# The block scales of the gate and up weight rows in a PSUM bank in place of SBUF

## Chip, cores, metric

One NeuronCore of a Trainium2 chip runs the whole program in one launch. The metric is the time of one execution on the device in microseconds (us). Float32 inputs and outputs; products are made of bfloat16 halves.

## What is computed

x is 4 x 2048 x 512. Each of the 8192 rows passes two blocks:

```
x = x + attention(layernorm(x), ctx, ctx)      # 16 heads of 32, 77 keys per batch, padding mask, weights 512 x 512
x = x + fp4_linear(silu(fp4_linear(n, w_gate)) * fp4_linear(n, w_up), w_down)     # n = layernorm(x), inner width 1408
def fp4_linear(x, w): return fp4(x) @ fp4(w).T
def fp4(v):                                    # blocks of 16 along the last dimension
    scale = max(max(abs(block)) / 6, 1e-12)
    return nearest of (0, .5, 1, 1.5, 2, 3, 4, 6) to abs(block / scale), with its sign, * scale
```

So the weights w_gate and w_up (1408 x 512 each) and w_down (512 x 1408) must be rounded once, block by block, and transposed, before the tiles of 128 rows of x can use them.

## The kernel before

**Stages.** There is a preparation (0 to 68 us) in which the attention weights, keys, values and w_down are transposed and rounded; a stretch (68 to about 190 us) in which the 11 pairs of gate and up rows (128 rows each of w_gate and w_up, index i) are rounded while the attention of the first tiles already runs; then a pipeline over the 64 tiles of 128 rows, whose steps repeat to the end. Each engine has one instruction queue, whose order is written out by hand; engines meet by semaphores alone.

**One pair of rows, i.** SyncE loads 128 x 512 of w_gate and of w_up into the two halves of `raw` (L319 to L321); it issues the load of pair i+1 once VectorE has divided both halves of pair i (semaphore `w_val`). VectorE's `weight_front(i)` does for both halves (two "jobs", alternating) `top` (L1258, the largest magnitude of each of the 32 blocks of 16), `scale` (L1264, a sixth of it), `inverse` (L1274, its reciprocal), and then `divide` (L1278: raw times the reciprocal, spread over each block, into `hv`). Each step of a job waits for the step before it of the same job. ScalarE's `weight_grid` squares the result (L926) and adds a large constant, by which it is rounded (L934). VectorE's `weight_end(i, half)` repeats the scale into a row of its own, `result_scale` (L1269), and subtracts (L1320). GpSimd's `weight_end` subtracts once more (L560) and multiplies by that last scale (L564), into `hq`. TensorE transposes `hq` (L715) into PSUM bank 0 or 1, ScalarE copies it out as the high bfloat16 half (L973), VectorE's `gate_up_low` takes the low half (L1246, wguT<-psum). L1246 is the line of a helper, `low`, which many steps use: `half_low` (halves<-...) and `probabilities_low` (p_h<-probs,p_h) too.

The scales stand in `w_sc` (SBUF, 128 x 2 jobs x 4 rows x 44 blocks): row 0 the largest magnitudes, 1 the scale, 2 the reciprocal, 3 the scale for GpSimd. The rows of w_down, in the preparation, use it too.

**What stands between.** VectorE's queue from 68 us on mixes the 11 fronts and 22 ends with the steps of tiles 0 to 3: statistics of the normalisation (L1390, L1394), `q_low` (L1399, L1402), `maximum` of the scores (L1432), `probabilities_low`, `normalised` (L1407, L1411), `half_low`, `residual` (L1448, x_new). The transposes between the stages go by DMA from SyncE's queue (t_room<-halves). TensorE starts the pipeline's gate and up products when the last low half of the weights is there.

**PSUM.** Eight banks of 128 x 512 float32. Bank 6 (`down_ps`) takes one of eight turns in the preparation, and from tile step 2 on the output of the last product; between the two nothing uses it.

Of the kernel before, what the change touches and what calls it, by code (L numbers as in the profile page):

```python
# [16 lines left out]
FP4_BLOCK = 16  # L17
# [8 lines left out]
def at_least(eng, sem, value):  # L26

    if not isinstance(value, int) or value > 0:
        eng.wait_ge(sem, value)
# [5 lines left out]
Job = namedtuple("Job", "name source src val sq mag tot res sc nb divided squared done")  # L35
# [29 lines left out]
def xattn_fp4_ffn_kernel(nc, x, ctx, mask, wq, bq, wk, bk, wv, bv, wo, bo, w_gate, w_up, w_down, out):  # L65
    BATCH, SEQ, D = x.shape
# [4 lines left out]
    KC = D // P  # L71
# [15 lines left out]
    HALF = INNER // 2  # L87
# [14 lines left out]
    with ExitStack() as es:  # L102
        def sb(name, shape, dt=F32):
            return es.enter_context(nc.sbuf_tensor(name, shape, dt))
# [11 lines left out]
        pv_ps = psum[:, 2:6, 0:GROUPS * VW].rearrange("p r (g w) -> p r g w", g=GROUPS)  # L116
        down_ps = bank[6]
        q_bank = o_bank = bank[7]
        quarter = [slice(r * DK, (r + 1) * DK) for r in range(GH)]


# [52 lines left out]
        w_sc = sb("w_sc", [P, 2, 4, HALF // FP4_BLOCK])  # L174
# [64 lines left out]
        fills = [entry for entry in plan if entry[0] not in ("quant", "round")]  # L239
# [413 lines left out]
        def _(pe):  # L653
# [10 lines left out]
            for n, (kind, what) in enumerate(fills):  # L664
                ps = bank[n % 8]
                at_least(pe, prep_lo, n - 7)
                if kind == "weight":
                    which, _, kc = what
                    if which not in waited:
                        waited.add(which)  # L670
# [570 lines left out]
        def _(dve):  # L1241
            own = Steps(dve, dve_step)

            def low(dst, ps, high, signal, value):

                return own.did(dve.tensor_tensor(dst, ps, high, ALU.subtract), signal, value)  # L1246
# [19 lines left out]

            def result_scale(job):

                own.did(dve.tensor_scalar(job.sc[:, 3, 0:job.nb], job.sc[:, 0, 0:job.nb], 1.0 / 6.0,  # L1269
                                          SCALE_FLOOR, ALU.mult, ALU.max))  # L1270

            def inverse(job):
# [3 lines left out]
            def divide(job):  # L1276
                own.after(marks[job.name])
                step_of(job, dve.scalar_tensor_tensor(blocks(job.val), blocks(job.src), TIES_DOWN, spread(job.sc, 2, job.nb),  # L1278
                                                      ALU.mult, ALU.mult), job.divided)
# [12 lines left out]
                step_of(job, dve.tensor_tensor(blocks(job.res), blocks(job.tot), spread(job.sc, 1, job.nb), ALU.mult),  # L1292
                        job.done)

            def weight_job(name, cols, divided, squared, done):
                part = [t[:, cols] for t in (raw, hv, h_sq, hm, hs, hq)]
                return Job(name, None, *part, w_sc[:, name], (cols.stop - cols.start) // FP4_BLOCK,
                           divided, squared, done)

            def weight_jobs(width, before):  # L1300

                return [weight_job(s, slice(s * width, (s + 1) * width),
                                   *((sem, before + (s + 1)) for sem in (w_val, w_grid, w_sum)))
                        for s in range(2)]

            def weight_start(jobs, before):

                at_least(dve, w_sum, before)
                for step in (top, scale, inverse):
                    for job in jobs:  # L1310
                        step(job)
                for job in jobs:
                    divide(job)

            def weight_sum(job, before):

                at_least(dve, w_quant, before - 1 + job.name)
                result_scale(job)
                dve.wait_ge(*job.squared)
                own.did(dve.tensor_tensor(job.tot, job.mag, job.val, ALU.subtract), *job.done)  # L1320


            n = 0
            for kind, what in plan:
                if kind == "quant":
                    dve.wait_ge(w_loaded, 16 * (what + 1))
                    weight_start(weight_jobs(HALF, 2 * what), 2 * what)
                    continue
                if kind == "round":
                    for job in weight_jobs(HALF, 2 * what):  # L1330
                        weight_sum(job, 2 * what)
                    continue
                if kind == "keys" and what == 0:
                    dve.wait_ge(bias_loaded, 16 * 3)
                    own.did(dve.tensor_scalar(bk_col[:], bk_col[:], SM_SCALE, None, ALU.mult), bk_ready, 1)
                ps = bank[n % 8]
                dve.wait_ge(prep_hi, n + 1)
                if kind == "weight":
                    which, dst, kc = what
                    own.did(dve.scalar_tensor_tensor(dst[:, LO, kc, :], ps[:], fill_scale[which], dst[:, HI, kc, :],  # L1340
                                                     ALU.mult, ALU.subtract), prep_lo, n + 1)
                elif kind == "ctx":
                    low(ctxT[:, LO, what], ps[:, 0:BATCH * KEYS], ctxT[:, HI, what], prep_lo, n + 1)
                elif kind == "keys":
                    own.did(dve.scalar_tensor_tensor(
                        k_all[:, :, LO, what, :], ps[:, 0:BATCH * KEYS].rearrange("p (b k) -> p b k", b=BATCH),
                        bk_col[:, what:what + 1], k_all[:, :, HI, what, :], ALU.add, ALU.subtract), prep_lo, n + 1)
                elif kind == "values":
                    low(v_all[:, what, LO, :, 0:DK], ps[0:KEYS, :].rearrange("p (h d) -> p h d", d=DK),
                        v_all[:, what, HI, :, 0:DK], prep_lo, n + 1)  # L1350
                elif kind == "down":
                    i, m = what
                    ks, cols = h_fills[m], slice(i * P, (i + 1) * P)
                    low(wdT[:, LO, ks.start:ks.stop, cols],
                        ps[:, 0:len(ks) * P].rearrange("p (k n) -> p k n", k=len(ks)),
                        wdT[:, HI, ks.start:ks.stop, cols], prep_lo, n + 1)
                else:
                    dve.wait_ge(bo_loaded, 16)
                    own.did(dve.tensor_tensor(bo_all[:], bo_all[:], wo_bv, ALU.add), prep_lo, n + 1)
                n += 1  # L1360
# [6 lines left out]
                    wguT[:, half, HI, :, cols], w_lo, 2 * i + half + 1)  # L1367

            def gate_up_jobs(i):
                return weight_jobs(D, 2 * i + 2 * KC)  # L1370

            def weight_front(i):

                dve.wait_ge(w_loaded, 32 * i + 16 * KC + 32)
                weight_start(gate_up_jobs(i), 2 * i + 2 * KC)

            def weight_end(i, half):
                weight_sum(gate_up_jobs(i)[half], 2 * i + 2 * KC)
# [9 lines left out]
            def first_norm(m):  # L1388
                dve.wait_ge(x_loaded, 16 * m + 16)
                marks["norm1"] = own.did(dve.bn_stats(ln1_stats_sb, x_in))  # L1390
# [73 lines left out]
            def step(e, d, f, a, b, n, m):  # L1464
# [62 lines left out]
                    h_chunk(f, 3)  # L1527
                own.restart()

            weight_front(0)  # L1530
            first_norm(0)
            first_norm_end(0)
# [228 lines left out]
```

## Time and profile before

| what | us |
|---|---|
| three timed runs | 2031.81, 2033.88, 2034.55; median 2033.88 |
| the profiled execution, its own time | 2031.19 |
| its span, first to last instruction | 2029.3 |
| TensorE busy | 1898.9 (94%) |
| VectorE busy | 1770.0 (87%) |
| ScalarE busy | 1266.9 (62%) |
| GpSimd busy | 448.8 (22%) |

The rows are of the profiled execution; 1.9 us of its time lie outside the span. Engines: PE is TensorE's matmuls, PEld its weight loads, DVE VectorE, ACT ScalarE, POOL GpSimd, SP SyncE. L1278 is line 1278 of the kernel. "out<-in" are the kernel's names; where a row names h_room, it is one of the tensors hv, hm, hs, hq that lie in it. A duration reaches from an instruction's start to the acknowledgement of its last write, so that two neighbours on one engine overlap by some 0.08 us. The idle time of an engine before an instruction is in brackets, with what ended it.

### The profile page before, as it was taken

The numbers are of one execution on the slowest core, as the hardware profiler recorded it, in microseconds if no ns is written. First come the engines' busy times: TensorE is split into PE (matmuls) and PEld (weight loads), VectorE is DVE, ScalarE is ACT, GpSimd is POOL, SyncE is SP. The second block draws the span as 40 slices with busy tenths as digits, with TensorE's granted clock in tenths as the row PEclk, the third lists the DMA queues.
The fourth block names the chain that finished last, engine by engine and source line by source line (L and its number), as shares of the span: only waits on it lengthen the run. The fifth ranks groups of instructions, "written<-read, shape, count | busy, mean of one in ns | idle before, by whom it ended". The sixth has DMA issues, their size and how long they took to land.

```text
span 2029.3 us, 48669 instructions
## 1 busy us (share of the span) xinstructions
PE 1898.9 (94%) x17724; PEld 1192.0 (59%) x17792; DVE 1770.0 (87%) x2676; ACT 1266.9 (62%) x2613; POOL 448.8 (22%) x526
## 2 busy tenths in 40 slices
PE   6446899999999999999999999999999999999987
PEld 4334566656665666656665666666665666666643
DVE  7898889888899889888899889888899889888874
ACT  4575766676666666676666666676667666676421
POOL 5554221122112221122112211222112211222100
PEclk8667999999999999999999999999999999999998
DMA  5344566565766566566666566556765566556623
GB/s 170 105 114 95 109 144 144 127 132 132 156 133 132 130 145 139 129 133 134 149 138 132 130 147 138 127 134 136 154 131 132 130 149 137 126 134 133 128 56 84
DMA packets 716996, 265.34 MB, mean 131 GB/s; under 512 B 667930, under 2 KB 669878, under 8 KB 716958
## 3 DMA queue, kind: packets, MB, share of 16 engines
q1 hardware_dynamic: 715374, 264.85, 58.9%
q8 instruction: 22, 0.36, 0.1%
q10 hardware_dynamic: 1584, 0.01, 0.1%
q14 instruction: 16, 0.13, 0.0%
HBM read 66.34 MB, written 34.86 MB: 50 GB/s over the span
## 4 chain that ended last, share of the span: by engine, by line
PE 86%; DVE 6%; DMA 3%; issue 2%; POOL 1%; SPq 1%; ACT 1%; DVEq 0%; POOLq 0%; another core or an unknown queue 0%; ACTq 0%
PE psum L724 44%; PE psum L660 38%; PE psum L737 2%; PE psum L766 2%; DMA t_room<-halves 1%; DVE h_room L1278 1%; SPq L345 1%; PE psum L755 1%; POOL h_room L560 1%; DVE w_sc L1258 1%; POOL h_room L564 1%; DMA ph_room<-h_room 1%; DVE wguT L1246 1%; DVE h_room L1320 0%; DMA q_room<-in_L_xattn_Wk_dram 0%
## 5 line engine op out<-in xcount | busy, mean ns | idle before, releaser
L724 PE MATMUL psum<-wguT,t_room 128*128 128x352 bf16 x6144 | 943.1, 314 | 15.5 <-DVE h_room L1426 9.0
L724 PEld LDWEIGHTS psum<-wguT,t_room 128*128 128x128 bf16 x6144 | 597.4, 98 | 346.4 <-DVE h_room L1426 10.4
L660 PE MATMUL psum<-wdT,ph_room 128*128 128x512 bf16 x2108 | 469.8, 381 | 11.2 <-DMA ph_room<-h_room 10.9
L581 POOL TENSOR_TENSOR ln_var_eps<-ln_mean_var,eps 128x1 f32<-128x1 f32 x128 | 103.8, 811 | 1185.7 <-DVE ln_mean_var L1394 998.6
L660 PEld LDWEIGHTS psum<-wdT,ph_room 128*128 128x128 bf16 x2112 | 207.6, 98 | 263.3 <-issue 17.4
L982 ACT ACTIVATE silu_g<-psum 128x352 f32<-128x352 f32 x256 | 117.4, 459 | 380.2 <-PE psum L724 377.1
L988 ACT ACTIVATE probs<-psum,neg_max 128x77 f32<-128x77 f32 x1024 | 244.3, 350 | 3.7 <-DVE neg_max L1432 3.0
L1426 DVE TENSOR_TENSOR h_room<-silu_g,psum 128x352 f32<-128x352 f32 x256 | 132.2, 517 | 81.3 <-ACT silu_g L982 81.1
L1019 ACT ACTIVATE t_room<-psum,bq_col 128x128 bf16<-128x128 f32 x256 | 72.9, 367 | 185.7 <-PE psum L660 185.7
L660 PE MATMUL psum<-t_room,wqT 128*128 128x128 bf16 x3072 | 187.6, 222 | 0.8 <-DMA t_room<-halves 0.8
L660 PEld LDWEIGHTS psum<-t_room,wqT 128*128 128x128 bf16 x3072 | 177.7, 100 | 1.5 <-DMA t_room<-halves 1.1
L660 PE MATMUL psum<-woT,t_room 128*128 128x512 bf16 x705 | 165.7, 384 | 12.0 <-issue 10.1
L926 ACT ACTIVATE h_sq<-h_room 128x1408 bf16<-128x1408 f32 (+2 forms) x94 | 108.1, 1150 | 96.3 <-DVE h_room L1278 96.3
L595 POOL TENSOR_TENSOR io_room<-io_room,bo_all 128x512 f32<-128x512 f32 x64 | 81.7, 1276 | 239.7 <-DMA io_room<-in_x_dram 239.7
L660 PEld LDWEIGHTS psum<-woT,t_room 128*128 128x128 bf16 x768 | 70.7, 99 | 84.3 <-issue 4.4
L1448 DVE TENSOR_TENSOR x_new<-psum,io_room 128x512 f32<-128x512 f32 x64 | 44.2, 691 | 81.9 <-PE psum L660 74.0
L1278 DVE SCALAR_TENSOR_TENSOR h_room<-h_room,h_sc 128x1408 f32<-128x1408 f32 x64 | 104.5, 1633 | 2.1
L1292 DVE TENSOR_TENSOR h_room<-h_room,h_sc 128x1408 f32<-128x1408 f32 x64 | 104.0, 1625 | 2.1
L1246 DVE TENSOR_TENSOR h_room<-h_room 128x1408 bf16<-128x1408 f32 x64 | 103.6, 1619 | 1.4 <-ACT h_room L1059 1.4
L1246 DVE TENSOR_TENSOR p_h<-probs,p_h 128x624 bf16<-128x624 f32 x128 | 103.9, 812 | 0.0
L1288 DVE SCALAR_TENSOR_TENSOR h_room<-h_sq,h_room 128x1408 f32<-128x1408 bf16 x64 | 103.6, 1618 | 0.1
L1258 DVE TENSOR_REDUCE h_sc<-h_room 128x88 f32<-128x1408 f32 x64 | 102.6, 1603 | 0.1
(105 smaller groups left out, 2498.8 us busy)
## 6 DMA issues: line engine op xcount, KB each, us to landing
io_room<-in_x_dram SPq DMA_DIRECT2D x128, 256.0 KB, 2.8
x_scratch<-x_new SPq DMA_DIRECT2D x64, 256.0 KB, 2.0
x_cur<-x_scratch SPq DMA_DIRECT2D x64, 256.0 KB, 3.3
out_dram<-io_room SPq DMA_DIRECT2D x64, 256.0 KB, 2.4
t_room<-halves SPq DMA_TRANSPOSE x192, 3.2
raw<-in_L_ffn_w_down_dram SPq DMA_DIRECT2D x4, 704.0 KB, 4.3
raw<-in_L_ffn_w_gate_dram SPq DMA_DIRECT2D x11, 256.0 KB, 2.7
raw<-in_L_ffn_w_up_dram SPq DMA_DIRECT2D x11, 256.0 KB, 2.9
```

Of the source, the lines that this page charges most:

```text
L581: own.did(pool.tensor_tensor(var_eps, mean_var[:, 1:2], eps[:], ALU.add))
L660: ins = pe.matmul(dst, left(i), right(j), start=first and n == 0, stop=last and n == len(PRODUCTS) - 1)
L724: ins = pe.matmul(ps[:, 0:CW], left[:, i, kc, :], wguT[:, which, j, kc, cols], start=(kc == 0 and i == j), stop=(kc == KC - 1 and i == LO))
L926: act.activation(dst, val, ACT.Square, scale=GRID_SLOPE).then_inc(done, 1)
L982: act.activation(silu_g[:, c % 2, :], gate_ps[c][:, 0:CW], ACT.Silu).then_inc(silu_done, 1)
L988: ins = act.activation(probs[:, h, 0:KEYS], score_ps[:, r, g, :], ACT.Exp, bias=neg_max[:, h:h + 1])
L1246: return own.did(dve.tensor_tensor(dst, ps, high, ALU.subtract), signal, value)
L1258: step_of(job, dve.tensor_reduce(job.sc[:, 0, 0:job.nb], blocks(job.src), AX_X, ALU.max, apply_absolute_value=True))
L1278: step_of(job, dve.scalar_tensor_tensor(blocks(job.val), blocks(job.src), TIES_DOWN, spread(job.sc, 2, job.nb), ALU.mult, ALU.mult), job.d ...
L1288: step_of(job, dve.scalar_tensor_tensor(job.tot, job.sq, GRID_BASE, job.tot, ALU.add, ALU.subtract))
L1292: step_of(job, dve.tensor_tensor(blocks(job.res), blocks(job.tot), spread(job.sc, 1, job.nb), ALU.mult), job.done)
L1426: own.did(dve.tensor_tensor(h[:, c * CW:(c + 1) * CW], silu_g[:, c % 2, :], up_ps[c][:, 0:CW], ALU.mult), h_done, f * CHUNKS + (c + 1))
```

## The change

The rows 0, 1 and 2 of the scales of gate and up rows move to bank 6 of PSUM, as `row_sc` (128 x 2 jobs x 3 rows x 32 blocks). Row 3, which GpSimd reads, stays in `w_sc`. The rows of w_down stay as they are. Before the first front, VectorE waits for the last fill of the preparation, since bank 6 was in use there.

```
+        row_sc = down_ps[:, 0:2 * 3 * (D // FP4_BLOCK)].rearrange("p (n r k) -> p n r k", n=2, r=3)
...
             def result_scale(job):
-                own.did(dve.tensor_scalar(job.sc[:, 3, 0:job.nb], job.sc[:, 0, 0:job.nb], 1.0 / 6.0,
+                own.did(dve.tensor_scalar(w_sc[:, job.name, 3, 0:job.nb], job.sc[:, 0, 0:job.nb], 1.0 / 6.0,
                                           SCALE_FLOOR, ALU.mult, ALU.max))
...
-            def weight_job(name, cols, divided, squared, done):
+            def weight_job(name, scales, cols, divided, squared, done):
                 part = [t[:, cols] for t in (raw, hv, h_sq, hm, hs, hq)]
-                return Job(name, None, *part, w_sc[:, name], (cols.stop - cols.start) // FP4_BLOCK,
+                return Job(name, None, *part, scales[:, name], (cols.stop - cols.start) // FP4_BLOCK,
                            divided, squared, done)
-            def weight_jobs(width, before):
-                return [weight_job(s, slice(s * width, (s + 1) * width),
+            def weight_jobs(scales, width, before):
+                return [weight_job(s, scales, slice(s * width, (s + 1) * width),
...
-                    weight_start(weight_jobs(HALF, 2 * what), 2 * what)
+                    weight_start(weight_jobs(w_sc, HALF, 2 * what), 2 * what)
...
-                    for job in weight_jobs(HALF, 2 * what):
+                    for job in weight_jobs(w_sc, HALF, 2 * what):
...
             def gate_up_jobs(i):
-                return weight_jobs(D, 2 * i + 2 * KC)
+                return weight_jobs(row_sc, D, 2 * i + 2 * KC)
...
+            dve.wait_ge(prep_lo, len(fills))
             weight_front(0)
```

## Rows read from the trace of the kernel before

**Rows 1.** The page: busy us, share of the span and count of each engine.

```profile
PE 1898.9 (94%) x17724; PEld 1192.0 (59%) x17792; DVE 1770.0 (87%) x2676; ACT 1266.9 (62%) x2613; POOL 448.8 (22%) x526
```

**Rows 2.** Windows: length, then busy us of each engine, clock, DMA.

```profile
68.00:182.00 114.00, 52.16 (x574) 39.06 (x576) 111.22 (x216) 72.19 (x160) 67.44 (x60) 0.63 0.41 97
230.00:1960.00 1730.00, 1711.87 (x16289) 1070.61 (x16349) 1536.34 (x2281) 1120.54 (x2315) 336.46 (x418) 1.00 0.62 134
```

**Rows 3.** Chain of waits, 68 to 182 us, shares by line.

```profile
by line: DVE h_room L1278 16.6%; DVE w_sc L1258 11.0%; DVE wguT L1246 9.0%; DVE h_room L1320 7.9%; DVE w_sc L1264 6.1%; DMA raw<-in_L_ffn_w_up_dram 5.3%; DVE w_sc L1274 4.5%; DVE halves L1246 4.4%; issue 4.4%; PE psum L660 4.3%; DMA t_room<
```

**Rows 4.** VectorE's groups, 68 to 180 us: busy us, mean ns, idle before.

```profile
L1278 DVE SCALAR_TENSOR_TENSOR h_room<-raw,w_sc 128x512 f32<-128x512 f32 x22 | 20.9, 991 | 0.0
L1320 DVE TENSOR_TENSOR h_room<-h_room 128x512 f32<-128x512 f32 x22 | 15.0, 680 | 0.4 <-ACT h_room L934 0.4
L1246 DVE TENSOR_TENSOR wguT<-psum,wguT 128x512 bf16<-128x512 f32 x22 | 14.7, 673 | 0.0
...
L1264 DVE TENSOR_SCALAR w_sc<-w_sc 128x32 f32<-128x32 f32 x22 | 8.7, 435 | 0.0
L1269 DVE TENSOR_SCALAR w_sc<-w_sc 128x32 f32<-128x32 f32 x22 | 6.5, 296 | 0.0
```

**Rows 5.** Timeline of VectorE, first front: start, us taken.

```profile
68.53 1.27 DVE L1258 TENSOR_REDUCE w_sc<-raw 128x32 f32<-128x512 f32 x2
69.72 0.30 DVE L1264 TENSOR_SCALAR w_sc<-w_sc 128x32 f32<-128x32 f32 x2
...
70.41 1.22 DVE L1278 SCALAR_TENSOR_TENSOR h_room<-raw,w_sc 128x512 f32<-128x512 f32 x2
71.55 0.69 DVE L1390 BATCH_NORM_STATS2 ln_stats<-io_room 128x6 f32<-128x512 f32 x1
```

**Rows 6.** Timeline, third front (i = 2), VectorE and GpSimd.

```profile
84.52 1.06 POOL L564 TENSOR_TENSOR h_room<-h_room,w_sc 128x512 f32<-128x512 f32 x1
84.77 0.93 DVE L1264 TENSOR_SCALAR w_sc<-w_sc 128x32 f32<-128x32 f32 x2
...
86.13 2.71 DVE L1278 SCALAR_TENSOR_TENSOR h_room<-raw,w_sc 128x512 f32<-128x512 f32 x2
86.90 1.39 POOL L564 TENSOR_TENSOR h_room<-h_room,w_sc 128x512 f32<-128x512 f32 x1
```

**Rows 7.** Timeline behind the front of i = 7, VectorE and GpSimd.

```profile
135.72 1.72 POOL L595 TENSOR_TENSOR io_room<-io_room,bo_all 128x512 f32<-128x512 f32 x1
136.22 1.28 DVE L1246 TENSOR_TENSOR wguT<-psum,wguT 128x512 bf16<-128x512 f32 x2
```

**Rows 8.** Timeline, 142 to 153 us: L1269 of i = 7, and x_new.

```profile
142.14 1.03 DVE L1269 TENSOR_SCALAR w_sc<-w_sc 128x32 f32<-128x32 f32 x1
...
152.48 0.69 DVE L1448 TENSOR_TENSOR x_new<-psum,io_room 128x512 f32<-128x512 f32 x1 [1.17 <-PE psum L660]
```

**Rows 9.** Chain of waits, 142 to 153 us: start, us.

```profile
142.33 4.76 DMA t_room<-halves
147.54 4.92 PE psum L660 x11
```

**Rows 10.** VectorE's groups, 230 to 1960 us.

```profile
L1292 DVE TENSOR_TENSOR h_room<-h_room,h_sc 128x1408 f32<-128x1408 f32 x60 | 97.5, 1625 | 2.0
L1399 DVE SCALAR_TENSOR_TENSOR t_room<-psum,bq_col,t_room 128x128 bf16<-128x128 f32 x177 | 51.2, 345 | 21.9 <-ACT t_room L1019 21.9
L1274 DVE RECIPROCAL h_sc<-h_sc 128x88 f32<-128x88 f32 x61 | 42.3, 694 | 0.1
L1274 DVE RECIPROCAL x_sc<-x_sc 128x32 f32<-128x32 f32 x61 | 21.5, 353 | 2.1
L1407 DVE RECIPROCAL inv_sum<-psum 128x16 f32<-128x16 f32 x60 | 15.4, 257 | 0.8 <-PE psum L737 0.8
```

**Rows 11.** ScalarE's groups, 68 to 180 us.

```profile
L934 ACT ACTIVATE h_room<-h_sq 128x512 f32<-128x512 bf16 x22 | 13.9, 630 | 0.7
L1026 ACT ACTIVATE psum<-mask_raw 128x1232 f32<-128x1232 uint8 x4 | 4.9, 1226 | 0.0
```

## The prediction

> **What bounds the kernel now.** I read the page first. VectorE is busy 87% of the span and GpSimd 22% [rows 1], but those are averages over stages with different limits. The windows part them. From 230 to 1960 us TensorE is busy 1711.9 of 1730 us: it is the bound there, and nothing that VectorE gains in that stage would move the end. The edit does nothing there anyway. From 68 to 182 us, where the gate and up rows are rounded, VectorE is busy 111.2 of 114 us and TensorE only 52.2 [rows 2]. The chain of waits says the same with names: in that stretch it runs over L1278, L1258, L1246, L1320, L1264, all VectorE, with two loads of raw and a piece of TensorE between [rows 3]. So a microsecond taken off VectorE in this stretch moves the start of the pipeline, and with it the end, unless another wait has taken its place by then.
>
> The groups of VectorE show what is odd in it. L1264 works on 32 numbers per partition and takes 435 ns on average; L1278 on 512 numbers takes 991 ns, where L1320 of the same width takes 680 [rows 4]. The timeline explains it. In the first front GpSimd has no rounding work yet: two L1264 take 0.30 us, two L1278 1.22 us, and the front is 71.55 - 68.53 = 3.02 us long [rows 5]. In the third front the pair of L1264 starts at 84.77, while GpSimd's L564 runs until 84.52 + 1.06 = 85.58, and ends at 85.70; the pair of L1278 starts at 86.13 and is over at 88.84, 0.55 us after the L564 that ends at 88.29 [rows 6]. The last of each kind that was held is finished its own length, or a little more, after a GpSimd instruction ends. An instruction of VectorE whose tensors all lie in SBUF is held until GpSimd's current one is done. Not so with a tensor in PSUM: two wguT<-psum take 1.28 us right within GpSimd's 135.72 to 137.44 [rows 7], and all 22 of them average 673 ns, as fast as the undisturbed L1320 [rows 4]. L1258 and L1274 are not held in any front.
>
> **What it removes.** All 11 fronts stand in the timeline of the same view as rows 5 and 6. From the first L1258 to the start of what follows the last L1278 they take, in order, 3.02, 4.99, 5.18, 4.24, 4.82, 3.65, 4.42, 5.35, 3.65, 3.92 and 3.26 us. The ten behind the first exceed it by 13.3 us in all. The groups give the same: 22 x (991 - 650) ns = 7.5 us for L1278 (two undisturbed ones span 1.22 us with an overlap of 0.08, so 650 ns each) and 22 x (435 - 175) = 5.7 us for L1264 [rows 4, 5]. With the reciprocals in PSUM, L1278 has one tensor in SBUF as input and one in PSUM, as the wguT row has; L1264 has none in SBUF. So all of the 13.3 us goes from where it stands.
>
> L1269 is held too (22 x (296 - 170) = 2.8 us) and also frees itself, but I cost this at nothing: L1320 stands right behind it with both inputs in SBUF, and it will be held in its place. The L1269 of rows 8 takes 1.03 us and is over at 143.17, when GpSimd has just finished, and the L1320 behind it runs free; with the edit L1320 waits for that same end.
>
> **What comes back.** GpSimd's four instructions per pair take about 4.7 us and begin when the first L1320 of a pair ends; the front that overlaps them will be over 1 us before them. What then follows matters. I went through the fronts one by one, moving each by the sum gained so far. i = 1: half_low (both inputs in SBUF) is held by the last L564; of 1.97 us I keep 1.76. i = 2: half_low follows directly and is held 1.6 us more; of 2.16 I keep 0.55. i = 3: 1.19 of 1.22. i = 4, 5, 6: statistics, maxima and wguT follow, which read PSUM or one tensor, or probabilities_low at a time when GpSimd is free: all of 1.80, 0.63 and 1.40. i = 7: the two probabilities_low land within GpSimd's L595 and wait for ScalarE's casts as well; of 2.33 I keep 1.5. i = 8: beside it runs another way to x_new, from half_low of tile 0's o: a DMA of 4.76 us, and TensorE's projection takes 4.92 us, and VectorE already waits 1.17 us for that at x_new [rows 8, 9]; so what VectorE gains between 142 and 152 us (0.63 us) only makes this wait longer. i = 9, 10: 0.90 and 0.24 us. Sum: 1.76 + 0.55 + 1.19 + 1.80 + 0.63 + 1.40 + 1.5 + 0 + 0.90 + 0.24 = 9.97, say 10.0 us. The loads of raw move with the divides that release them, so they hide nothing and cost nothing.
>
> **What it adds.** 8 instructions per front and 2 per pair of ends now touch PSUM, 110 in all. No instruction of VectorE writes PSUM in this trace, so its price must be bounded. Low end: nothing. Reading PSUM at 512 elements costs no more than SBUF (673 against 680 ns, rows 4). The reciprocal takes 353 ns for 32 and 694 ns for 88 numbers, 6.1 ns each, so 16 in SBUF would take 256 ns, and 16 read from PSUM take 257 [rows 10]. For writing, only ScalarE has rows: 630 ns for 512 elements into SBUF, 1226 for 1232 into PSUM; the difference is 596 ns for 720 elements, 0.83 each, which leaves 206 ns of fixed time in both [rows 11]. High end: the short L1399, 128 elements, 345 ns. From L1320 (512 elements, 680 ns) and L1292 (1408, 1625 ns) an element costs 945 / 896 = 1.055 ns; that leaves a fixed part of 345 - 135 = 210 for L1399, against 680 - 540 = 140 for L1320, 0.07 us more, though L1399 has a per-partition operand besides [rows 4, 10]. I take 0.02 us per instruction, near the reciprocal's row, the only other small operation: 110 x 0.02 = 2.2 us; between nothing and 7.7 us. The added wait at 68.5 us stands in an idle-free place behind the last wdT fill and exposes its acknowledgement, the overlap of two neighbours: 0.08 us, as between 69.80 (68.53 + 1.27), where L1258 ends, and 69.72, where L1264 starts [rows 5]. TensorE and ScalarE don't touch bank 6 in the stretch.
>
> Net: 10.0 - 2.2 - 0.1 = 7.7 us. Against the profiled execution's 2031.2 that is 2023.5. That one lies at the low end of the times; from the median of 2033.9 the forecast is 2026.2 us.
>
> A rule speaks against the edit. The Trainium skill, "VectorE: DVE Perf Modes", in its section on the TRN2 errata, puts VectorE's fixed part at 58 cycles from SBUF and 120 from PSUM; 62 cycles at 0.96 GHz are 65 ns, an estimate of 7.1 us for 110 instructions, and a gain of 2.8 us, 2031.1, in place of 7.7. The rows of reads at 16 and 512 elements disagree with it; for writes no row decides.
>
> **Rivals.**
> (a) Small operations on PSUM pay the high end, 0.07 us: 110 x 0.07 = 7.7 us, net 10.0 - 7.7 - 0.1 = 2.2 us, 2031.7. For it: L1399. Against it: the reciprocal from PSUM. Chance 0.13. The rule above would bring this case.
> (b) The gain is given back more often than I counted: each front's early end meets GpSimd's chain or a wait for ScalarE at the next step, as in i = 2 and 7. With half of the kept 10 us: 5 - 2.3 = 2.7 us, 2031.2. Against it: in i = 3 to 6 the steps behind read PSUM. Chance 0.08.
> (c) The edit doesn't free L1278: with raw in SBUF it is held like before, and only L1264 gains. L1264's share is 5.7 of 13.2 us, so 4.3 of the 10 us would remain, less 2.3: 2.0 us, 2031.9. Against it: wguT<-psum,wguT, which has one tensor in SBUF too. Chance 0.04.
> (d) Slower: a write into PSUM is acknowledged late, and here each step waits for the one before it (L1258 to L1264 to L1274 to L1278), with nothing but the other job between. In rows 5 the second L1264 follows the end of the second L1258 at once, so there is no slack to hide it in. From 0.09 us per instruction (9.9 / 110) on the change is a loss; at 0.13, nearly twice (a)'s price, it costs 14.3 us, 4.4 more than the 9.9: 2038.3. Against it: ScalarE's rows 11. Chance 0.07.
>
> **How the numbers follow.** My own case has 0.68. Its gain lies between 10.0 - 0.1 - 0 = 9.9 and some 4.5 (0.05 us each). The timed runs here lie up to 2.7 us apart, so 0.2% (4.1 us) is about what can be told from no change. The range reaches from 2022.0, the gain with PSUM free and a little of L1269 and of the last fronts added, over (a), (b) and (c) to 2033.0; beyond it are (d) and a little more. Faster by over 0.2%: my case but for its weak end (0.65), and those ends of (a) and (b) that gain more, 0.68. Within: the rest of my case, (a), (b) and (c), 0.25. Slower: (d), 0.07.
>
> **What would show it.** L1278 at about 650 ns, L1264 at 180 to 220, all fronts 3.0 to 3.4 us long though GpSimd works beside them; half_low behind the front of i = 2 held by about 1.2 us; some L1320 held at over 1 us where L1269 was; more than 1.17 us of idle time before x_new at 152 us; GpSimd's L564 nearer to 1.06. The pipeline's first gate and up product would start 7 to 8 us earlier than 190.4, and everything behind it would keep its distance. The forecast is wrong if fronts are over 3.6 us long (rivals a and d), if L1278 still shows 1.5 us (c), or if the fronts are short and the pipeline doesn't start earlier (b).

## The result, and the profile after

The changed kernel takes 2020.26 us (median of 4 runs, 2019.79 to 2022.32), the kernel before 2033.05 (4 runs beside it, 2031.81 to 2034.55): a ratio of 0.9939 with a 95% interval of 0.9922 to 0.9956. That is 12.8 us or 0.6% less where 7.7 were forecast, and 1.7 us below the low end of the range. Line numbers behind the added line are one higher than before: L1279 is what L1278 was, L1265 was L1264, and so on.

The page after, first of it the span, then the engines' busy time against [rows 1]:

```profile
span 2017.9 us, 48669 instructions
...
PE 1894.5 (94%) x17724; PEld 1189.1 (59%) x17792; DVE 1758.7 (87%) x2676; ACT 1266.9 (63%) x2613; POOL 446.9 (22%) x526
```

The profiled execution's time is 2019.79 us. Its span is 11.4 us shorter than the 2029.3 of before, and VectorE is busy 11.3 us less. The windows, against [rows 2]; the first one now ends where the rounding does, at 169.2:

```profile
68.00:169.20 101.20, 48.85 (x574) 37.18 (x576) 99.51 (x216) 72.00 (x160) 65.50 (x60) 0.66 0.46 109
230.00:1950.00 1720.00, 1702.40 (x16128) 1063.79 (x16186) 1528.27 (x2267) 1112.63 (x2300) 334.20 (x414) 1.00 0.62 134
```

The same 216 instructions of VectorE take 99.5 us in place of 111.2, and the stretch that holds them is 101.2 us in place of 114. The pipeline behind is what it was: TensorE fills 99% of it. VectorE's groups in the stretch, 68 to 167.2 us, against [rows 4] (busy us, mean ns, idle before):

```profile
L1321 DVE TENSOR_TENSOR h_room<-h_room 128x512 f32<-128x512 f32 x22 | 17.3, 788 | 0.5 <-ACT h_room L935 0.4
L1247 DVE TENSOR_TENSOR wguT<-psum,wguT 128x512 bf16<-128x512 f32 x22 | 14.8, 676 | 0.0
L1259 DVE TENSOR_REDUCE psum<-raw 128x32 f32<-128x512 f32 x22 | 14.1, 684 | 1.1 <-DMA raw<-in_L_ffn_w_up_dram 0.7
L1279 DVE SCALAR_TENSOR_TENSOR h_room<-raw,psum 128x512 f32<-128x512 f32 x22 | 13.9, 674 | 0.0
...
L1275 DVE RECIPROCAL psum<-psum 128x32 f32<-128x32 f32 x22 | 6.2, 330 | 0.0
L1270 DVE TENSOR_SCALAR w_sc<-psum 128x32 f32<-128x32 f32 x22 | 3.9, 177 | 0.0
...
L1265 DVE TENSOR_SCALAR psum<-psum 128x32 f32<-128x32 f32 x22 | 3.6, 194 | 0.0
```

L1279 fell from 991 to 674 ns, L1265 from 435 to 194, L1270 from 296 to 177. L1321 rose from 680 to 788: part of L1270's hold stands there now. All eleven fronts are 3.05 to 3.15 us long, and their sum fell from 46.5 to 33.9 us. One of the four executions of one_column_psum, in the table below, took 3982.78 us and is left out of its median.

In the chain of waits behind the stretch, the block of 72 gate and up products that follows the first h_chunk starts 12.6 us earlier than the 190.41 of before (24 such products stand ahead of that h_chunk in both kernels):

```profile
177.81 12.23 PE psum L725 x72
```

### The profile page after: what moved, and what is told of

Same layout as the page of the kernel before. It is cut to its first block, busy times and chain, and to the rows that moved or that the text cites. A ratio compares the mean times of both kernels' runs of the same rounds, so it can differ in the third digit from the quotient of the medians.

```text
span 2017.9 us, 48669 instructions
## 1 busy us (share of the span) xinstructions
PE 1894.5 (94%) x17724; PEld 1189.1 (59%) x17792; DVE 1758.7 (87%) x2676; ACT 1266.9 (63%) x2613; POOL 446.9 (22%) x526
## 4 chain that ended last, share of the span: by engine, by line
PE 85%; DVE 6%; DMA 3%; issue 2%; POOL 1%; SPq 1%; ACT 1%; DVEq 0%; POOLq 0%; another core or an unknown queue 0%; ACTq 0%
PE psum L725 43%; PE psum L661 37%; PE psum L738 2%; PE psum L767 2%; DMA t_room<-halves 1%; SPq L346 1%; PE psum L756 1%; POOL h_room L561 1%; DVE h_room L1321 1%; DVE psum L1259 1%; POOL h_room L565 1%; DVE h_room L1279 1%; DMA ph_room<-h_room 1%; DMA q_room<-in_L_xattn_Wk_dram 0%; DVE wguT L1247 0%
## 5 line engine op out<-in xcount | busy, mean ns | idle before, releaser
L661 PE MATMUL psum<-wdT,ph_room 128*128 128x512 bf16 x2108 | 469.9, 381 | 11.1 <-DMA ph_room<-h_room 10.9
L1279 DVE SCALAR_TENSOR_TENSOR h_room<-h_room,h_sc 128x1408 f32<-128x1408 f32 x64 | 104.8, 1638 | 2.2
```

Of the source, the lines that this page charges most:

```text
L661: ins = pe.matmul(dst, left(i), right(j), start=first and n == 0, stop=last and n == len(PRODUCTS) - 1)
```

## The experiments

Each stretch below is read from that run's timeline: from the start of the first front to the start of the first h_chunk (L1426 before), 68.53 to 189.83 us in the kernel before, so 121.30. The rest is the span less that second start. Times are medians, with the ratio to the kernel before run beside them (2032.38, 2032.26 and 2032.62 us in the three sets).

```
kernel           us       ratio (95%)              stretch  11 fronts  rest
before           2033.05  1                        121.30   46.5       1839.5
after            2020.26  0.9939 (0.9922, 0.9956)  108.64   33.9       1840.7
before_again     2031.58  0.9999 (0.9990, 1.0008)  122.10   46.0       1838.8
after_again      2021.43  0.9946 (0.9933, 0.9960)  108.69   33.9       1840.9
recip_only       2022.06  0.9952 (0.9938, 0.9966)  113.02   39.4       1837.5
max_only         2028.26  0.9980 (0.9971, 0.9989)  118.57   42.2       1841.5
one_column_sbuf  2010.54  0.9893 (0.9878, 0.9908)  100.62   33.7       1842.0
one_column_psum  2011.28  0.9903 (0.9885, 0.9921)  101.28   34.3       1841.0
wait_only        2031.87  1.0000 (0.9990, 1.0009)  121.32   46.0       1841.2
down_too         2022.21  0.9952 (0.9939, 0.9966)  108.75   33.8       1841.2
split_before     2026.99  0.9972 (0.9960, 0.9984)  115.40   40.6       1841.1
split_after      2014.76  0.9917 (0.9904, 0.9931)  106.31   33.9       1837.4
quarter_after    2020.92  0.9941 (0.9928, 0.9955)  112.17   33.9       1837.9
front8_sbuf      2020.84  0.9948 (0.9933, 0.9964)  110.25   34.4       1840.2
```

### Both kernels again

> The kernel before, unchanged, profiled a second time. It tells how much of the 12.6 us by which the pipeline started earlier in the changed kernel is chance. Theory (the way has its own fixed length): from the end of half_low of tile 0's o to the start of x_new (L1448) it takes 10.3 us again, as in the first profile (142.22 to 152.48), and the wait of 1.2 us before x_new is there again; the first silu product h_chunk (L1426) starts at 189.8 within 0.5. Rival (its length varies by itself, with the landing of the DMA transpose and the clock that TensorE is granted at that moment): 8.4 to 10.3 us, and the pipeline starts up to 2 us earlier. Time 2033 in both within 1.5.

> The changed kernel, unchanged, profiled a second time. Fixed way: from the end of half_low of tile 0's o to x_new 8.4 us again (131.96 to 140.33) and no wait before x_new; first h_chunk (L1427) at 177.2 within 0.5; time 2020.3. Rival (length varies by itself): up to 10.3 us, x_new waits, and the first h_chunk starts up to 1.8 us later, time up to 2022.3. Where both repeat, the shorter way belongs to the changed kernel and has a cause in it.

The two differ by 10.2 us here (by 11.0 from the other runs of the kernel before in this set) and by 12.8 in the first set, while their stretches differ by 13.41 and 12.66. So the size of the gain is known to one or two microseconds. The stretch repeats within 0.1 us for the changed kernel and 0.8 for the other; front8_sbuf below shows that it can also move by 1.1 us with nothing changed. Both sets lie above the forecast's 7.7. The idle time before x_new is there again in before_again (1.75 us) and again missing in after_again; before_again's first h_chunk came at 190.75, outside of the expected 189.8 within 0.5.

### One step alone in PSUM

The rows of the scales are picked one by one: recip_only has the reciprocals (row 2, what L1278 reads) in PSUM, max_only the block maxima (row 0, what L1264 and L1269 read). The edit of recip_only, against the changed kernel; max_only has (0,) in place of (2,):

```diff
+            def gate_up_scales(name):
+                return Rows([(row_sc if row in (2,) else w_sc)[:, name, row] for row in range(3)])
...
-                return weight_jobs(row_sc, D, 2 * i + 2 * KC)
+                return weight_jobs(gate_up_scales, D, 2 * i + 2 * KC)
```

> Only the reciprocals (row 2) stand in PSUM; the largest magnitudes and the scale stay in SBUF. Hold theory (an instruction whose tensors all lie in SBUF waits for GpSimd's current instruction, no other): L1278's like falls to 675 ns, L1264's like stays held once per front (mean 400 to 480 ns), fronts 3.5 to 4.2 us long, gain about 7.5 / 13.2 of 12.6 us: 7 us, time 2026. Rival (the saved time meets GpSimd's chain at the next step, as the prediction had it): gain under 4 us, time over 2029.

> Only the largest magnitudes (row 0) stand in PSUM; scale and reciprocal in SBUF. L1264's and L1269's likes then read PSUM and aren't held (under 220 ns), L1278's like is as before. Shares simply add: gain 5.7 / 13.2 of 12.6 us = 5.4 us, time 2027.6. Hold theory in full: the freed L1264 lets L1278 start earlier into the same GpSimd instruction or the one before, so part of the hold only moves to it: L1278's like over 1000 ns, fronts 4.0 to 4.6 us, gain 2 to 4 us, time 2029 to 2031.

VectorE's groups of recip_only, 66.8 to 168 us:

```profile
L1289 DVE SCALAR_TENSOR_TENSOR h_room<-raw,psum 128x512 f32<-128x512 f32 x22 | 13.9, 673 | 0.0
...
L1275 DVE TENSOR_SCALAR w_sc<-w_sc 128x32 f32<-128x32 f32 x22 | 8.6, 430 | 0.0
```

and of max_only, 66.8 to 175 us:

```profile
L1289 DVE SCALAR_TENSOR_TENSOR h_room<-raw,w_sc 128x512 f32<-128x512 f32 x22 | 22.2, 1049 | 0.0
L1337 DVE TENSOR_TENSOR h_room<-h_room 128x512 f32<-128x512 f32 x22 | 17.4, 790 | 0.4 <-ACT h_room L945 0.4
...
L1275 DVE TENSOR_SCALAR w_sc<-psum 128x32 f32<-128x32 f32 x22 | 3.5, 185 | 0.0
```

Each step is freed by the place of its own operand: the divide falls to 673 ns with its scales in PSUM although raw stays in SBUF, so rival (c) is out. The shares aren't equal: the divide's alone shortens the stretch by 8.3 us against the 121.3 of the profile before, the maxima's alone by 2.7. In max_only the divide is held longer than before (1049 against 991 ns), since it comes up earlier, while GpSimd is still at work. In its third front the divides come up at 83.76 and are over at 86.24, 0.55 us after the L571 of GpSimd that runs from 83.97 to 85.69. What is freed first in a row of steps hands part of its hold to the next one.

The timed runs part the two kernels less well than the stretches do. recip_only's median is 10.3 us below the kernel before where 7 were expected, and 0.6 above the changed kernel, though its stretch is 4.3 us longer than that one's. Its profiled execution (2019.32 us) was the fastest of its five, with a rest 3 us shorter than the changed kernel's; the last section has one cause of that. max_only's 4.1 us stand beside 2.7 of stretch, within the 2 to 4 that were expected where a hold moves on.

### No GpSimd beside the fronts: the price of PSUM alone

GpSimd's subtraction and product of the rounding work on one column in place of 512; the other 511 columns of the rounded values are left out. In one_column_sbuf the scales are in SBUF, in one_column_psum in PSUM.

```diff
             def gate_up_end(i, half):
...
+                col = slice(half * D, half * D + 1)
...
+                own.did(pool.tensor_tensor(hs[:, col], hm[:, col], hs[:, col], ALU.subtract), w_sub, at)
...
+                own.did(pool.tensor_tensor(hq[:, col], hs[:, col], w_sc[:, half, 3, 0:1], ALU.mult), w_quant, at)
```

> Leaves out: GpSimd's subtraction and multiplication of the gate and up rows are done on one column of 512 alone. GpSimd then hardly works in the stretch, and all scales stand in SBUF. Theory (holds by GpSimd's current instruction are the whole excess): L1264's like 170 to 185 ns, L1278's 650 to 675, all fronts 3.0 to 3.1 us long with the scales in SBUF. Rival (part of the excess is something else, such as loads or ScalarE): fronts stay over 3.3 us in places. Since half_low, p_h and L1320 are not held either, the first h_chunk comes earlier than in the changed kernel: 13 + 5 us before 189.8.

> Leaves out the same, with the scales in PSUM as in the changed kernel. No hold is left in either, so the difference of the two is the bare price of the 110 instructions on PSUM. Theory (price about 0.007 us each, from the first front: 3.09 against 3.01 us): 0.8 us later at the first h_chunk. The prediction's 0.02 us each: 2.2 us. The rule's 0.065 us each: 7.1 us.

VectorE's groups of one_column_sbuf, 68.5 to 160 us:

```profile
L1288 DVE SCALAR_TENSOR_TENSOR h_room<-raw,w_sc 128x512 f32<-128x512 f32 x22 | 13.5, 653 | 0.0
...
L1274 DVE TENSOR_SCALAR w_sc<-w_sc 128x32 f32<-128x32 f32 x22 | 3.7, 198 | 0.0
```

and of one_column_psum, 67 to 160 us:

```profile
L1289 DVE SCALAR_TENSOR_TENSOR h_room<-raw,psum 128x512 f32<-128x512 f32 x22 | 13.9, 674 | 0.0
...
L1275 DVE TENSOR_SCALAR psum<-psum 128x32 f32<-128x32 f32 x22 | 3.6, 194 | 0.0
```

Two things follow. With the scales in SBUF, and GpSimd nearly out of the way, the fronts are 3.0 us each but for one of 3.53 (33.7 in all). In that one the small steps meet the addition of 512 columns, L605, which GpSimd still does in this kernel:

```profile
119.18 1.26 POOL L605 TENSOR_TENSOR io_room<-io_room,bo_all 128x512 f32<-128x512 f32 x1
119.81 0.76 DVE L1274 TENSOR_SCALAR w_sc<-w_sc 128x32 f32<-128x32 f32 x2
```

They are over 0.13 us after it. So the excess of 13 us was the hold by GpSimd, all of it. And the pair differs by 101.28 - 100.62 = 0.66 us of stretch for 110 instructions: 0.006 us each, and less than two profiles of one kernel can differ by. Reading the 32 reciprocals, each spread over 16 numbers, from PSUM makes the divide 21 ns longer. The 62 cycles that the Trainium skill gives as the difference of the fixed part between a source in SBUF and one in PSUM ("VectorE: DVE Perf Modes", the section on the TRN2 errata) would be 7.1 us by the prediction's estimate for all 110, and 5.7 us for the 88 of them that read PSUM; the measurement decides against them.

The stretch of one_column_sbuf is 20.7 us shorter than that of the kernel before, where 18 were expected. The pair also says what the changed kernel still loses: 108.64 against 101.28 us, some 7 us, in holds outside the fronts and in waits for GpSimd.

### The added wait, and the rest of the rounding

wait_only adds to the kernel before the one wait of the change. down_too has, beside the change, the scales of the down rows in bank 6, which leaves the fills seven banks.

```diff
+            dve.wait_ge(prep_lo, len(fills))
```

```diff
-                ps = bank[n % 8]
+                ps = fill_banks[n % 7]
...
-                    weight_start(weight_jobs(w_sc, HALF, 2 * what), 2 * what)
+                    weight_start(weight_jobs(row_sc, HALF, 2 * what), 2 * what)
```

> The kernel before with only the added wait for the last fill ahead of the first front. Both theories: 0.06 to 0.1 us, no difference in time (2032.4 within 1.5), the first front starts 0.06 us later behind the last wdT fill. Besides, a third profile with the scales in SBUF: the DMA of tile 0's o lands after 4.8 to 5.3 us if this belongs to the kernel before, 3.2 us at times if it is chance.

> The changed kernel, and in the preparation too the scales of the w_down rows in bank 6 (rows 0 to 2), the fills turning through the seven other banks. Held there before: L1264 at 412 ns and L1269 at 176, 8 each. Theory (a freed instruction gains where VectorE or GpSimd behind it is on the chain): L1264's like to about 200 ns, 8 x 0.2 = 1.6 us less, of which at most 1 us reaches the first front (it starts at 68.6). Rival (one bank fewer makes TensorE wait for its fill): the first front starts later than 68.6, time over 2021.4. Time 2020.5 by the first, 2022 to 2024 by the second.

The wait costs nothing that can be seen (stretch 121.32 against 121.30 and 122.10). The down rows gain nothing either: 2022.21 stands beside 2021.43 for the changed kernel in the other set, and the first front starts no earlier than in other profiles (67.65 us; 66.95 to 69.31 in the rest).

### GpSimd's instructions in parts

If VectorE is held until GpSimd's current instruction ends, shorter ones hold it for less. Both instructions of the rounding are cut into two of 256 columns (split_before on the kernel before, split_after on the changed one) or four of 128 (quarter_after).

```diff
+                parts = [slice(half * D + n * wide, half * D + (n + 1) * wide) for n in range(2)]
+                for n, cols in enumerate(parts):
+                    last = n == 2 - 1
+                    own.did(pool.tensor_tensor(hs[:, cols], hm[:, cols], hs[:, cols], ALU.subtract),
+                            *((w_sub, at) if last else ()))
```

> The kernel before, with GpSimd's subtraction and multiplication of the gate and up rows each issued as two instructions of 256 columns in place of one of 512. Theory (VectorE is held to the end of GpSimd's current instruction and gets in between two of them): the holds get about half as long, L1278's like from 975 ns to 800 or so, L1264's from 435 to 320, first front to first h_chunk 121.3 us becomes 116 to 118. Rival (it is held until GpSimd's chain of four is over, as the prediction took it for half_low): L1278's and L1264's like as long as before or longer, since the chain gets longer, and 121 to 124 us.

> The changed kernel with the same split in two. What is still held there (L1320's like 788 ns on average, p_h 1045, half_low 966 and 1122, in all some 7 us) shrinks by nearly half by the theory: first front to first h_chunk from 108.7 to 105.5 to 107, time 2018.5 to 2020. By the rival (chain) 108.7 or more, time 2021.5 and over.

> The changed kernel, split in four instructions of 128 columns. Theory: holds shorter still, but GpSimd's fixed time per instruction (some 0.15 us) lengthens its chain by 2 us per pair, so that more of VectorE's instructions meet it: 105 to 108 us from first front to first h_chunk. Rival: over 109.

VectorE's groups of split_before, 68.8 to 173 us: the divide lost a third of its excess (from 991 ns), the small step two thirds (from 435), with nothing but GpSimd's instructions changed.

```profile
L1294 DVE SCALAR_TENSOR_TENSOR h_room<-raw,w_sc 128x512 f32<-128x512 f32 x22 | 18.6, 884 | 0.0
...
L1280 DVE TENSOR_SCALAR w_sc<-w_sc 128x32 f32<-128x32 f32 x22 | 5.2, 272 | 0.0
```

GpSimd's groups of quarter_after, 68 to 175 us:

```profile
L584 POOL TENSOR_TENSOR h_room<-h_room 128x128 f32<-128x128 f32 x88 | 44.8, 539 | 3.6 <-DVE h_room L1337 2.6 <-PE psum L732 1.0
L593 POOL TENSOR_TENSOR h_room<-h_room,w_sc 128x128 f32<-128x128 f32 x88 | 37.5, 456 | 1.7
```

Halves help both kernels: the stretch is 5.9 us shorter on the one, 2.3 on the other. In split_before it comes out at 115.40, just below the expected 116 to 118, though the divide lost less than expected (884 ns, not 800); split_after's 106.31 lies within its range.

Quarters don't help, and their expectation failed: 112.17 us where 105 to 108 were expected. That is in the range of the rival, over 109, but the cause is another. A quarter of the width takes 0.54 us where the whole took 1.44, so GpSimd works 82 us on the two steps and waits only 5.3 before them. VectorE is busy 98.2 us of the stretch, less than the 102.5 of the changed kernel, but the stretch is 3.5 us longer: VectorE now waits, in part for GpSimd's product, as it never does in the changed kernel. L1286 is result_scale, which writes the scale that the product reads. From its waits, 69 to 182 us (us in total, times, longest):

```profile
DVE w_sc L1286 <- POOL h_room L593: 2.2, 3, 1.2
```

split_after is the fastest kernel that computes all: 2014.76 us, 18 less than before. That is less than the 2018.5 to 2020 expected, and not all of it is from the split, as the last section shows.

### Is a front free that lies beside the way to x_new?

The prediction counted the front of i = 8 at nothing. front8_sbuf is the changed kernel with that one front back in SBUF.

```diff
-                return weight_jobs(row_sc, D, 2 * i + 2 * KC)
+                return weight_jobs(w_sc if i == 8 else row_sc, D, 2 * i + 2 * KC)
```

> The changed kernel, with the scales of the pair i = 8 alone in SBUF, so its front is held again (3.65 in place of 3.07 us). The prediction costs this at nothing, since the way of tile 0's o to x_new was to set that moment: first front to first h_chunk 108.7 us as in the changed kernel, x_new at the same place. By the profiles of the changed kernel VectorE arrives at x_new no earlier than TensorE: 109.2 to 109.4 us, the DMA of o landing after 3.2 us. Third possibility: the DMA lands after 4.8 us or more as in the kernels with held fronts, and x_new comes 1 to 2 us later.

The front is 3.65 us long, 0.56 more than in the changed kernel, and the stretch 110.25 us, 1.6 longer, outside of the 108.7 and the 109.2 to 109.4 that were expected; the DMA of o landed after 3.1 us, so the third possibility isn't it either. But only a part of this is the front's. Counted from the start of the first front, the front of i = 8 begins after 66.46 us, and after 65.36 and 65.31 in the two profiles of the changed kernel, with no difference in the code up to there: 1.1 us were lost before, half of it at i = 1 (a wait of 0.64 us for raw) and half at i = 2 (a longer half_low). From the start of this front to the next it takes 7.53 us against 6.98 and 7.16, and from there to h_chunk 36.26 against 36.30 and 36.22. The half_low behind the front isn't held, and nothing waits before x_new (VectorE's timeline of front8_sbuf, 136 to 141.5 us):

```profile
138.38 0.68 DVE L1247 TENSOR_TENSOR halves<-io_room,halves 128x512 bf16<-128x512 f32 x1
```

So the front isn't free: its hold of some 0.6 us costs 0.4 to 0.55 us, about itself and no more. The timed runs (2020.84) can't tell this from the changed kernel's 2021.43 in another set; it rests on one profile against two.

## Why the prediction was right, and where it was wrong

**Right: the bound, the cause, the excess.** VectorE sets the stretch, GpSimd's hold is the excess of the fronts, and PSUM operands take all of it away: 12.6 us of the fronts' 13.3 are gone. The hold of L1269 reappeared in L1320, now L1321, as forecast: 22 x (296 - 177) = 2.6 us less on the one, 22 x (788 - 680) = 2.4 us more on the other. One such L1321 in the timeline of the changed kernel, 87.6 to 92 us, is over at 89.77, 0.56 us after the L561 that runs until 89.21:

```profile
87.95 1.26 POOL L561 TENSOR_TENSOR h_room<-h_room 128x512 f32<-128x512 f32 x1 [1.05 <-DVE h_room L1321]
88.40 0.17 DVE L1270 TENSOR_SCALAR w_sc<-psum 128x32 f32<-128x32 f32 x1
88.50 1.27 DVE L1321 TENSOR_TENSOR h_room<-h_room 128x512 f32<-128x512 f32 x1
```

**Too wide: which instructions are held.** The prediction said that an instruction whose tensors all lie in SBUF is held. Two kinds in the fronts have all of them there and weren't, the block maximum and the reciprocal. Their means in the kernel before, 68 to 180 us, are those of one_column_sbuf (677 and 321 ns), where GpSimd hardly works:

```profile
L1258 DVE TENSOR_REDUCE w_sc<-raw 128x32 f32<-128x512 f32 x22 | 14.0, 675 | 1.2 <-DMA raw<-in_L_ffn_w_up_dram 0.9
L1274 DVE RECIPROCAL w_sc<-w_sc 128x32 f32<-128x32 f32 x22 | 6.2, 324 | 0.0
```

The prediction noted this itself, and its sum holds nothing for them. What the runs show held are additions and products of two SBUF tensors and the tensor_scalar of 32 numbers.

**Wrong: the size.** The starts of the fronts in the two timelines give what each step kept, from the start of its front to the start of the next (for i = 10, to the start of h_chunk), beside what the prediction kept of it:

```
i         0      1     2     3     4     5     6     7     8     9     10
kept    -0.10  1.70  1.99  1.14  1.80  0.72  1.29  1.86  1.81  0.82  -0.37
forecast   0   1.76  0.55  1.19  1.80  0.63  1.40  1.5   0     0.90   0.24
```

With -0.06 ahead of i = 0 they sum to 12.60, the price of PSUM and the wait included. The forecast's 9.97 didn't include them; they took 2.3 off. Seven steps agree within 0.2 us. Four terms failed: i = 2 (+1.44), i = 8 (+1.81), the price of PSUM (2.2 was forecast, 0.66 measured), and, the other way, i = 10 (-0.61, where a probabilities_low takes 1.56 us in place of 0.80). The steps differ by 2.63 in all (with +0.36 of i = 7 and small ones), and the 2.3 that weren't to be taken off make it 4.9, the distance from 7.7 to 12.6.

**i = 2: half_low was not held 1.6 us more.** The timeline of the changed kernel, 83 to 86.2 us on VectorE:

```profile
83.23 0.33 DVE L1265 TENSOR_SCALAR psum<-psum 128x32 f32<-128x32 f32 x2
...
83.94 1.26 DVE L1279 SCALAR_TENSOR_TENSOR h_room<-raw,psum 128x512 f32<-128x512 f32 x2
85.12 0.86 DVE L1247 TENSOR_TENSOR halves<-io_room,halves 128x512 bf16<-128x512 f32 x1
85.91 0.68 DVE L1391 BATCH_NORM_STATS2 ln_stats<-io_room 128x6 f32<-128x512 f32 x1
```

and on GpSimd, 83 to 88 us:

```profile
83.14 1.06 POOL L565 TENSOR_TENSOR h_room<-h_room,w_sc 128x512 f32<-128x512 f32 x1
84.15 1.28 POOL L561 TENSOR_TENSOR h_room<-h_room 128x512 f32<-128x512 f32 x1
85.51 1.39 POOL L565 TENSOR_TENSOR h_room<-h_room,w_sc 128x512 f32<-128x512 f32 x1
```

The pair of L1279 ends at 85.20 as if GpSimd weren't there. half_low comes up while L561 runs, until 85.43, and is over at 85.98, 0.55 us later, the same distance as in [rows 6]; the next L565, from 85.51 on, is itself the longer one (1.39 us). So an instruction is held to the end of GpSimd's current instruction and gets in between two of them. The step that failed took GpSimd's chain for one block that lasts until its last L564. The prediction stated the rule itself and did not apply it here: half_low took 0.86 us, 0.18 more than L1391 beside it, and not 1.6 more.

How much it is held depends on where GpSimd stands, and a little luck is in the 0.18. front8_sbuf, whose code is the same here, has half_low come up just after the next L565 began (84 to 87 us):

```profile
84.47 1.06 POOL L565 TENSOR_TENSOR h_room<-h_room,w_sc 128x512 f32<-128x512 f32 x1
84.62 1.45 DVE L1247 TENSOR_TENSOR halves<-io_room,halves 128x512 bf16<-128x512 f32 x1
```

It is over at 86.07, 0.54 us after that L565, and was held for some 0.8 us: one instruction of GpSimd, and still only half of the 1.6.

The Trainium skill has this in "SBUF — State Buffer", section "Who interferes with whom": whoever issues first gets the shared pair of ports for the whole instruction, and an instruction of VectorE with at most one SBUF input, outside the modes that use both ports, doesn't contend. This trace agrees with both: half_low, with two SBUF inputs, was held to the end of L561, and L1279, with one, was not (674 ns), nor were L1258 and L1274. L1264 has one SBUF input too and was held (435 ns); that agrees only if it ran in one of those modes, which no run here shows.

**i = 8: the way to x_new isn't fixed.** From the end of o's half_low to the start of x_new it took 10.26 us before, 1.17 of them idle on VectorE; it takes 8.37 now, and nothing waits (10.83 and 8.54 us in the second profiles). VectorE's timeline of the changed kernel, 139 to 141.5 us, answers to [rows 8]:

```profile
139.73 0.68 DVE L1321 TENSOR_TENSOR h_room<-h_room 128x512 f32<-128x512 f32 x1
140.33 0.68 DVE L1449 TENSOR_TENSOR x_new<-psum,io_room 128x512 f32<-128x512 f32 x1
```

Two parts of that way got shorter. The projection, TensorE's timeline of the changed kernel, 134 to 141 us, against 4.92 us in [rows 9]:

```profile
135.99 4.29 PE L661 MATMUL psum<-woT,t_room 128*128 128x512 bf16 x11 [0.22 <-issue]
```

It goes with the clock that TensorE was granted. The windows of the projection, before and then after (the clock is the third number from the right):

```profile
147.54:152.46 4.92, 4.92 (x13) 1.97 (x13) 3.77 (x8) 4.54 (x13) 1.73 (x1) 0.50 0.78 200
135.99:140.28 4.29, 4.29 (x13) 1.76 (x13) 4.29 (x9) 3.67 (x10) 0.49 (x1) 0.59 0.87 217
```

In the other profiles the same projection took from 5.30 us at 0.50 (before_again) to 2.87 at 0.88 (one_column_sbuf); no fixed floor can be read from one of them.

And the DMA from half_low to t_room lands in 3.2 us where it took 4.76 [rows 9]. Over the fourteen profiles this landing has two values: 3.1 to 3.5 us in the eight whose fronts ahead of it are free of holds, but for the one of one_column_sbuf (both of the changed kernel, down_too, front8_sbuf, split_after, quarter_after and the one_column pair), 4.8 to 5.3 us in the six others. Why the short landing goes with the freed fronts was not settled: SyncE issues the same transfers in the same order in all of them, and no run changed the DMA alone. Even with 4.8 us recip_only has no idle time before x_new, since its VectorE comes to it later. The step that failed was to let the durations of a transfer and of a product, seen once, set a fixed floor: it put the gain of i = 8 at nothing, and 1.81 us were kept.

**The price of PSUM** was taken at 0.02 us each for want of a row and is 0.006. ScalarE's rows of [rows 11] could not have told it: one line through a point that writes SBUF and one that writes PSUM gives both the same fixed time by construction. Rivals (a) and (d), and the rule of 62 cycles, would have needed 0.065 and more. Rival (b) shows clearly in one place, i = 10, and in part at i = 7, where 2.27 us went from the front and 1.86 were kept. The added wait is within noise of its 0.1.

**What the end kept.** The stretch gained 12.66 us and the span 11.4: the rest is 1.2 us longer in the changed kernel's profile. No run shows what it is made of. The block of 72 products is 0.4 us shorter after than before, so it isn't that; but wait_only, with all scales in SBUF, has a rest of 1841.2 us, so a difference of this size needs no PSUM operand.

## What to carry to other kernels

Where a small operation shows several times the duration of an undisturbed one, look at what GpSimd runs at that moment: an addition, product or tensor_scalar of VectorE whose operands all lay in SBUF was held until GpSimd's current instruction ended (block maxima and reciprocals weren't), and moving its small operand to a free PSUM bank freed it for 6 ns apiece. Then ask which such instruction comes next, for it inherits the rest of the hold, and whether GpSimd's long instructions can be cut in two, which frees the ones that can't be moved, but not in so many parts that GpSimd becomes the limit. In a sum over steps, hold each instruction only to the end of GpSimd's current one, and do not take a transfer's landing time from a single row for a floor.

## What the runs showed of the hardware

**GpSimd's time by width.** Its subtraction takes 1439 ns on average for 512 columns with the scales in SBUF, holds of its own among them, 865 for 256 and 539 for 128: the first two rows are GpSimd's groups of the kernel before (68 to 180 us) and of split_after (67 to 170 us).

```profile
L560 POOL TENSOR_TENSOR h_room<-h_room 128x512 f32<-128x512 f32 x22 | 31.6, 1439 | 26.2 <-DVE h_room L1320 26.2
```

```profile
L584 POOL TENSOR_TENSOR h_room<-h_room 128x256 f32<-128x256 f32 x44 | 37.2, 865 | 11.1 <-DVE h_room L1337 11.1
```

Halving the width takes 40% off, so four parts cost 1.5 times the whole. This is the working of quarter_after's loss.

**The granted clock at the start of the pipeline.** The block of 72 gate and up products behind the first h_chunk took 12.61 us before, 12.23 after and 10.93 in split_after. The windows of 3.4 us from the start of that h_chunk, 0.6 us ahead of the block, of the changed kernel and then of split_after (length, busy us of TensorE, its loads, VectorE, ScalarE, GpSimd, then the clock):

```profile
177.20:180.60 3.40, 2.79 (x10) 1.48 (x11) 2.10 (x5) 1.52 (x2) 0.88 (x3) 0.52 0.85 175
```

```profile
173.70:177.10 3.40, 2.83 (x19) 1.88 (x20) 2.24 (x5) 1.52 (x2) 0.78 (x2) 1.00 1.15 213
```

At 0.52 (nearly all of it at 1.2 GHz) TensorE gets 10 records done, at 1.00 (2.4 GHz) 19. What clock it is granted there differs from profile to profile, and 1.3 to 1.7 us with it: recip_only and quarter_after have the clock of 1.00 and 10.9 us too and, like split_after, a rest of 1837.4 to 1837.9 us, where the others have 1838.8 to 1842.0. (max_only's block took 13.84 us, with 0.50 in its first window.) So part of split_after's lead (3.3 us of its rest) is not from its stretch, and a difference of two single spans below 2 us says nothing of an edit.
